# Feed-forward with a hidden width of 682: two 42-column remainders in one column block

## What is computed

```python
HID = int(DIM * 4 * 2 / 3)               # 682, DIM is 256
h = shift_token(x)
mu = h.mean(-1, keepdims=True)
var = h.var(-1, keepdims=True)
h = (h - mu) / jnp.sqrt(var + 1e-05) * lg + lb
h = h @ w1 + b1                          # w1: 256 x 1364
a, g = jnp.split(h, 2, axis=-1)          # linear half, gate
h = a * jax.nn.gelu(g, approximate=False)
x = x + h @ w2 + b2                      # w2: 682 x 256
```

## Time and profile before

| | us |
|---|---|
| median of 3 runs | 5164.81 (5160.68 to 5165.73) |
| profiled execution, span | 5174.7 |
| PE busy | 4715.5 (91%) |
| DVE busy | 3744.5 (72%) |
| ACT busy | 2880.2 (56%) |
| POOL busy | 1688.8 (33%) |
| up projection, gate blocks (L1994), 1152 matmuls | 303.2 |
| up projection, linear blocks (L1994), 1152 matmuls | 302.2 |
| down projection (L2008), 2304 matmuls | 284.9 |

### The profile page before, as it was taken

How to read it: one execution, slowest core, us unless ns; L and a number is a source line. 1 busy time by engine, 2 the same in 40 slices (tenths; PEclk the granted TensorE clock), 3 DMA queues, 4 the chain that set the end, 5 groups by cost and what they waited for, 6 DMA issues and landing times. The chain is left out here.

```text
span 5174.7 us, 97724 instructions
## 1 busy us (share of the span) xinstructions
PE 4715.5 (91%) x27802; PEld 2976.0 (58%) x27802; DVE 3744.5 (72%) x8989; ACT 2880.2 (56%) x6305; POOL 1688.8 (33%) x2440
## 2 busy tenths in 40 slices
PE   4779999999999986599999997999799999997998
PEld 2423332333323324477777775888677777776887
DVE  6978888888888849677777775554677777774554
ACT  1327666767776761366666664333566666663333
POOL 3610000000000004455555553333455555554554
PEclk8869999999999998799999998999899999998999
DMA  4753232332332317200000001111100000002221
GB/s 154 248 116 49 46 57 41 55 55 40 57 49 46 56 40 227 86 23 23 23 22 22 22 22 53 47 46 37 49 23 22 22 22 22 22 21 79 62 75 48
DMA packets 385590, 288.63 MB, mean 56 GB/s; under 512 B 64284, under 2 KB 346392, under 8 KB 385056
## 3 DMA queue, kind: packets, MB, share of 16 engines
q1 hardware_dynamic: 385056, 282.19, 22.7%
HBM read 178.74 MB, written 102.83 MB: 54 GB/s over the span
## 5 line engine op out<-in xcount | busy, mean ns | idle before, releaser
L949 DVE TENSOR_REDUCE fa_mx<-fa_pR 128x1 f32<-128x512 f32 x2048 | 1275.8, 683 | 207.1 <-PE fa_pR L826 202.1
L925 ACT ACTIVATE fa_P<-fa_pS 128x512 f32<-128x512 f32 x2048 | 1077.3, 600 | 530.1 <-PE fa_pS L849 527.0
L1558 POOL TENSOR_TENSOR wa_pn<-wa_pr,wa_ri 128x512 f32<-128x512 f32 x512 | 701.6, 1371 | 785.8 <-DVE wa_ri L1614 777.1
L826 PE MATMUL fa_pR<-fa_K,fa_Q 96*128 96x512 bf16 x2048 | 804.4, 394 | 28.9 <-DMA fa_K<-parts_d 28.4
L849 PE MATMUL fa_pS<-fa_Q,fa_K 98*128 98x512 bf16 x2048 | 784.2, 386 | 26.3 <-issue 21.8
L1179 POOL TENSOR_TENSOR ao_xn<-ao_xn,ao_mod 128x1024 f32<-128x1024 f32 x16 | 37.6, 2350 | 1739.9 <-DVE ao_xn L1144 1739.9
L1378 PE MATMUL wa_pS<-wa_kT,wa_qT 128*128 128x256 f32 x2048 | 567.3, 401 | 37.4 <-issue 34.4
L849 PEld LDWEIGHTS fa_pS<-fa_Q,fa_K 98*128 98x128 bf16 x2048 | 199.1, 98 | 637.7 <-ACT fa_P L925 439.0
L862 PE MATMUL fa_pO<-fa_P,fa_V 128*32 128x512 f32 x4096 | 551.7, 611 | 5.9 <-ACT fa_OT L914 5.2
L1495 ACT ACTIVATE wa_pr<-wa_sm,wa_mn 128x256 f32<-128x256 f32 x1024 | 512.7, 504 | 44.2 <-DVE wa_mn L1606 44.0
L1606 DVE CUSTOM_DVE_ANT_0 wa_sm<-wa_pS,wa_mask 128x256 f32<-128x256 f32 x1024 | 391.1, 419 | 143.2 <-issue 128.8
(11 more groups left out here) (191 smaller groups left out, 7547.7 us busy)
## 6 DMA issues: line engine op xcount, KB each, us to landing
parts_d<-pj_parts SPq DMA_DIRECT2D x96, 256.0 KB, 2.8
fa_Q<-parts_d SPq DMA_DIRECT2D x192, 128.0 KB, 4.5
fa_K<-parts_d SPq DMA_DIRECT2D x192, 128.0 KB, 7.2
v_d<-pj_v SPq DMA_DIRECT2D x16, 1024.0 KB, 6.0
fa_V<-v_d SPq DMA_DIRECT2D x32, 512.0 KB, 9.7
pj_x<-in_L_attn_x SPq DMA_DIRECT2D x16, 512.0 KB, 6.7
att_d<-fa_att SPq DMA_DIRECT2D x32, 256.0 KB, 3.2
ao_att<-att_d SPq DMA_DIRECT2D x16, 512.0 KB, 4.8
```

What stands on the lines that cost most here:

```text
L826: nc.tensor.matmul(row_tile(), Qs[0:SROWS, s, h, q * P:(q + 1) * P], Ks[0:SROWS, s, h, half * 512:(half + 1) * 512], start=True, stop=True ...
L925: nc.scalar.activation(Pr[:, k % 2, h, half * 512:(half + 1) * 512], pS[:, (s * exped.per + u) % T, :], ACT.Exp).then_inc(exped.sem, 1)
L949: nc.vector.tensor_reduce(mx[:, j // 2, j % 2:j % 2 + 1], row_tile(), AX.X, ALU.max).then_inc(row_free, 1)
L1558: nc.gpsimd.tensor_tensor(pn[:, hp % 2], pr[:, hp % 2], inv, ALU.mult).then_inc(s["weighted"].sem, 1)
```

## The change

The 42 last columns of the linear half and the 42 last of the gate go into one column block of `w1`: the linear ones at columns 0 to 41 of block 5, the gate ones at 64 to 105. For j = 5 PE makes this block alone, in `pG[:, 1]`, with six matmuls instead of twelve; rows 0 to 63 of it are the linear half, rows 64 to 127 the gate. ACT reads rows 64 to 127 and writes the gelu to rows 0 to 63 of `gl`; mix, `u_high` and the split of block 5 work on rows 0 to 63. Rows 64 to 127 of `u[:, :, 5]` are zeroed once for each layer. The gate half of `w1` is loaded by two transfers instead of one (640 columns and 42). `lifted` counts five for a chunk instead of six; the waits that asked for the end of the up projection by `lifted` now ask by `gated`; and PE waits for the sixth mix of the chunk before ahead of its second gate block, since that mix now reads `pG[:, 1]`.

```diff
-        gated=HB, lifted=HB, gelu=HB, mixed=HB, ...
+        gated=HB, lifted=HB - 1, gelu=HB, mixed=HB, ...
...
-        LOADS = 11
+        LOADS = 12
+        LAST = P // 2
...
+                    (w1_in[:, :, 0, 0:HID], w1_rows[:, :, 0:HID]),
+                    (w1_in[:, :, 1, 0:full], w1_rows[:, :, HID:HID + full]),
+                    (w1_in[:, :, 0, full + LAST:full + LAST + HL], w1_rows[:, :, HID + full:2 * HID]),
...
+                nc.vector.memset(u[LAST:P, :, HB - 1, :].bitcast(F32), 0.0).then_inc(zeroed, 1)
...
-                    dve.wait_ge(s["lifted"].sem, s["lifted"].upto(g(n), j + 1))
+                    if j < HB - 1:
+                        dve.wait_ge(s["lifted"].sem, s["lifted"].upto(g(n), j + 1))
...
+                    rows_, ps = (P, pA) if j < HB - 1 else (LAST, pG)
+                    nc.vector.scalar_tensor_tensor(out=uF[0:rows_, j % 2, :], in0=ps[0:rows_, j % 2, :],
+                                                   scalar=b1[0:rows_, 0, j:j + 1], in1=gl[0:rows_, j % 2, :],
...
+                            if half == 0 and j == HB - 1:
+                                continue
...
+                            if half == 1 and j == 1 and not (early(n, 1) and layer == 0):
+                                pe.wait_ge(s["mixed"].sem, s["mixed"].upto(g(n - 1)))
+                            part = half if j < HB - 1 else 0
...
+                    at, rows_ = (0, P) if j < HB - 1 else (LAST, LAST)
+                    nc.scalar.activation(gl[0:rows_, j % 2, :], pG[at:at + rows_, j % 2, :], ACT.Gelu,
+                                         bias=b1[at:at + rows_, 1, j:j + 1]).then_inc(s["gelu"].sem, 1)
```

More of the change, by code:

```diff
@@ L1727, in ffn_signals @@
         chain=LN_INCS, normed=1, biased=2, turned=1, hT_ready=2 * KT, h_split=1,
-        gated=HB, lifted=HB, gelu=HB, mixed=HB, u_high=HB, u_split=HB, y_done=1, summed=1, scaled=1, final=1,
+        gated=HB, lifted=HB - 1, gelu=HB, mixed=HB, u_high=HB, u_split=HB, y_done=1, summed=1, scaled=1, final=1,
     )
@@ L1834, in _ @@
                 ]
[L1835 to L1838, removed]
+                w1_rows = a["L0_ffn_w1"][layer].rearrange("(k p) n -> p k n", p=P)
+                loads += [
+                    (w1_in[:, :, 0, 0:HID], w1_rows[:, :, 0:HID]),
+                    (w1_in[:, :, 1, 0:full], w1_rows[:, :, HID:HID + full]),
+                    (w1_in[:, :, 0, full + LAST:full + LAST + HL], w1_rows[:, :, HID + full:2 * HID]),
+                ]
                 for d_, s_ in loads:
@@ L1846, in _ @@
                                      row[0:full].rearrange("(k p) -> p k", p=P)).then_inc(w_in, 16)
-                        sp.dma_start(b1[0:HL, half, HB - 1:HB],
+                        sp.dma_start(b1[half * LAST:half * LAST + HL, half, HB - 1:HB],
                                      row[full:HID].rearrange("(p k) -> p k", k=1)).then_inc(w_in, 16)
@@ L1888, in mix @@
                     dve.wait_ge(s["gelu"].sem, s["gelu"].upto(g(n), j + 1))
-                    dve.wait_ge(s["lifted"].sem, s["lifted"].upto(g(n), j + 1))
+                    if j < HB - 1:
+                        dve.wait_ge(s["lifted"].sem, s["lifted"].upto(g(n), j + 1))
                     if not (early(n, 1) and layer == 0 and j < 2):
                         dve.wait_ge(s["u_split"].sem, g(n) * HB + j - 1)
-                    nc.vector.scalar_tensor_tensor(out=uF[:, j % 2, :], in0=pA[:, j % 2, :], scalar=b1[:, 0, j:j + 1],
-                                                   in1=gl[:, j % 2, :], op0=ALU.add,
-                                                   op1=ALU.mult).then_inc(s["mixed"].sem, 1)
+                    rows_, ps = (P, pA) if j < HB - 1 else (LAST, pG)
+                    nc.vector.scalar_tensor_tensor(out=uF[0:rows_, j % 2, :], in0=ps[0:rows_, j % 2, :],
+                                                   scalar=b1[0:rows_, 0, j:j + 1], in1=gl[0:rows_, j % 2, :],
+                                                   op0=ALU.add, op1=ALU.mult).then_inc(s["mixed"].sem, 1)
                 def split_h(n, p):
@@ L1899, in split_h @@
                     if not early(n, 2):
-                        dve.wait_ge(s["lifted"].sem, s["lifted"].upto(g(n - 2)))
+                        dve.wait_ge(s["gated"].sem, s["gated"].upto(g(n - 2)))
                     nc.vector.tensor_tensor(hT[:, p, 1], hF[:], hT[:, p, 0].bitcast(F32),
@@ L1955, in body @@
                         pool.wait_ge(s["u_high"].sem, s["u_high"].upto(g(n), j + 1))
-                        nc.gpsimd.tensor_tensor(u[:, 1, j, :], uF[:, j % 2, :], u[:, 0, j, :].bitcast(F32),
+                        rows_ = P if j < HB - 1 else LAST
+                        nc.gpsimd.tensor_tensor(u[0:rows_, 1, j, :], uF[0:rows_, j % 2, :],
+                                                u[0:rows_, 0, j, :].bitcast(F32),
                                                 ALU.subtract).then_inc(s["u_split"].sem, 1)
@@ L1974, in _ @@
                 pe.wait_ge(w_in, 16 * LOADS)
+                pe.wait_ge(zeroed, 4)
                 def turn(n, p):
@@ L1989, in up @@
                         for half, ps, done, freed in ((1, pG, "gated", "gelu"), (0, pA, "lifted", "mixed")):
+                            if half == 0 and j == HB - 1:
+                                continue
                             if not (early(n, 1) and layer == 0 and j < 2):
                                 pe.wait_ge(s[freed].sem, g(n) * HB + j - 1)
+                            if half == 1 and j == 1 and not (early(n, 1) and layer == 0):
+                                pe.wait_ge(s["mixed"].sem, s["mixed"].upto(g(n - 1)))
+                            part = half if j < HB - 1 else 0
                             products = [(k, x, y) for k in range(KT) for x, y in SPLIT_PRODUCTS]
                             for i, (k, x, y) in enumerate(products):
-                                last = nc.tensor.matmul(ps[:, j % 2, :], w1[:, x, k, half, j * P:(j + 1) * P],
+                                last = nc.tensor.matmul(ps[:, j % 2, :], w1[:, x, k, part, j * P:(j + 1) * P],
                                                         hT[:, p, y, k, :], start=(i == 0),
@@ L2042, in h_out @@
                     if not early(n, 2):
-                        act.wait_ge(s["lifted"].sem, s["lifted"].upto(g(n - 2)))
+                        act.wait_ge(s["gated"].sem, s["gated"].upto(g(n - 2)))
                     for k in range(KT):
@@ L2052, in gelu @@
                         act.wait_ge(s["mixed"].sem, g(n) * HB + j - 1)
-                    nc.scalar.activation(gl[:, j % 2, :], pG[:, j % 2, :], ACT.Gelu,
-                                         bias=b1[:, 1, j:j + 1]).then_inc(s["gelu"].sem, 1)
+                    at, rows_ = (0, P) if j < HB - 1 else (LAST, LAST)
+                    nc.scalar.activation(gl[0:rows_, j % 2, :], pG[at:at + rows_, j % 2, :], ACT.Gelu,
+                                         bias=b1[at:at + rows_, 1, j:j + 1]).then_inc(s["gelu"].sem, 1)
                 def u_high(n, j):
@@ L2059, in u_high @@
                         act.wait_ge(s["y_done"].sem, s["y_done"].upto(g(n - 1)))
-                    nc.scalar.copy(u[:, 0, j, :], uF[:, j % 2, :]).then_inc(s["u_high"].sem, 1)
+                    rows_ = P if j < HB - 1 else LAST
+                    nc.scalar.copy(u[0:rows_, 0, j, :], uF[0:rows_, j % 2, :]).then_inc(s["u_high"].sem, 1)
                 def body(n, p, following=True):
```

## The result

The changed kernel takes 5178.0 us (18 runs, 5171.4 to 5188.1) against 5164.8 (18 runs): ratio 1.0024, 95% interval 1.0017 to 1.0030. It is slower by 13 us, with 192 matmuls fewer (27802 to 27610).

The account below looks back on a forecast made before the run. PE was taken as full in layer 0, with DVE's hn ending together with its sixth linear block, and as waiting for hn in layer 1. -2.8 + 0.9 + 5.4 = +3.5 us on 5164.8 gave 5168; range 5159 to 5176.

Parts of the forecast that it names:

- hn is what the transposes wait for: Next chunk's transposes on PE: they wait for DVE's normalized hn, so the removed 1.40 us becomes waiting; 15 chunks per layer give 0.
- The rival in which it comes off by itself: Transposes in the first layer do not wait for hn and move up, 15 x 1.40 = 21 us, some 5147; chance 0.04.
- The last chunk of each layer: No transposes there, the down projection follows directly, so the block comes off: 2 x 1.40 = 2.8 us less.
- The start of each layer: The twelfth load, issued ahead of the small vectors, delays lb by 0.47 us per layer: +0.9 us for both.
- Registers, 64 rows, the new wait: In the chunk loops: extra DVE registers, 64-row instructions and PE's wait for the previous chunk's sixth mix, all taken at 0.
- No lost clock in layer 0: PE's new waits of 1.4 us before the first layer's transposes keep the upper clock: 0.
- that rival: The first layer loses the clock too, 1.43 us in each of 15 chunks, 21.5 us: 5193; chance 0.05.
- The order of DVE and GpSimd around hn: Rival: order tips around hn; second layer 11.4 us faster (5157) or first layer 14.3 slower (5182); chance 0.03 each.
- The clock in layer 1: Second layer's waits grow to 3.2 us; 10 of 12 lose the clock instead of six, 1.43 us each: +5.4 us.

Follow-up runs that it names:

- e8: The changed kernel run once more without an edit, for a second profile: 5176.6 us, ratio 1.0019.
- e2: The changed kernel with six matmuls of unread result in place of the removed block, in both layers: 5166.5 us, ratio 0.9998.
- e6: The changed kernel with hn written one mix earlier, behind the fourth mix and before the fifth: 5133.2 us, ratio 0.9930.
- e9: The changed kernel with the whole normalization behind the first three mixes, hn before the fourth: 5100.8 us, ratio 0.9871.
- e1: The kernel before run once more without an edit, for a second profile: 5164.7 us, ratio 0.9999.
- e4: The kernel before with only the gate half of w1 loaded in two transfers instead of one: 5165.9 us, ratio 1.0003.
- e10: The kernel before with the whole normalization behind the first three mixes, hn before the fourth: 5155.6 us, ratio 0.9980.
- e3: The kernel before with six matmuls added behind the last linear block of each chunk, layer 1 alone: 5169.1 us, ratio 1.0006.
- e7: The kernel before with hn written one mix earlier, behind the fourth mix and before the fifth: 5147.4 us, ratio 0.9958.
- e5: The changed kernel with three matmuls added behind the packed block, layer 1 alone: 5169.0 us, ratio 1.0005.

## Why the prediction was wrong

The likeliest time was 5168 and the range ended at 5176; measured were 5178.0 and, in e8, 5176.6. The chance for slower by more than 0.2% was 0.09.

- **hn is what the transposes wait for: right.** In layer 0 the wait is 1.38 us (1.4 predicted), in layer 1 3.1 to 3.3 (3.2), 1.3 to 1.7 in its first three chunks (1.4 to 1.8), the offset behind hn 0.14, the chunk 26.3. e2 shows that the removed block only turned into waiting, e6 and e9 that it comes off when hn comes earlier. The rival in which it comes off by itself is out.
- **The last chunk of each layer: right.** Layer 0 takes 435.1 us in three profiles of the changed kernel or with its layer 0, and 437.0 in e1: 1.9 less, of which 1.4 is the block. The rest comes with the twelfth load: in e4, which has nothing else, the first chunk is shorter too.
- **The start of each layer: the wait right, its effect smaller.** The wait for lb is about 0.5 us longer, predicted 0.47, but the first chunk gives most of it back.
- **Registers, 64 rows, the new wait: right**, nothing that e2 can tell (up to 3 us by its interval).
- **No lost clock in layer 0: right.** The mean is 1.00, and that rival is out.
- **The order of DVE and GpSimd around hn: not tipped.** hn takes 1.38 us in layer 0 and, from the fourth chunk on, 2.3 to 2.4 in layer 1, as before. The rival mechanism is real, though: moved by one mix, in e6, hn of layer 0 takes 2.42.
- **The clock in layer 1: the step that failed.** The term was +5.4 us, put together from ten losses in place of six, at 1.43 us. Two things were wrong in it. The larger is the base: six losses came from a single execution whose span lay 9.9 us above the median of the runs. (Its time was further off: in all other profiles the time is 1.7 to 1.9 us more than the span.) The prediction said "the sum is a difference and is carried over to the median". The six losses were themselves a part of that excess: e1, e2 and e4 have one. The other is the price. Losses after waits of 1.8 us cost 1.4 to 1.7; the six of the first profile cost 1.54 in the mean, and the prediction took one pair of chunks that gives 1.43. After 3.2 us seven of seventeen cost about 2.5 (30.75 against 28.29), with the down projection at 10.61 us instead of the 9.5 that it takes after the shorter wait. The count, ten, was near: nine and eight. In sum layer 1 takes 474.8 us in the mean of the two profiles after, against 461.1 in e1: +13.7, where -1.4 + 5.4 = +4.0 was predicted.

Put together from the profiles: -1.9 in layer 0, +13.7 in layer 1, +1.0 for the waits at the starts, +12.8 us. Measured were +13.3 and +11.0 (e8).

Had the profile of before been set beside its runs at this point, the range would have shown it: a term that rests on something that changes from execution to execution needs more than one execution as a base, or the assumption that the median has none of it (one loss in place of six makes the same ten losses worth 5.7 + 5 x 1.66 = 14 us, with which the sum gives 5177). The granted clock of the runs that were not profiled fits this. Twelve of 99 runs of the kernel before took 5173 us or more; the mean clock of the whole execution is on record for eleven of them, 0.951 to 0.953, while 70 others have 0.953 to 0.956 and the first profile 0.952. The 28 runs of the changed kernel have 0.947 to 0.953. So about one execution in eight of the kernel before seems to be like the first profile. That is read from the means; at how many waits those executions lost the clock was not seen, and why one does and the next doesn't stays open.

## What to carry to other kernels

Before work is taken off a full engine, look at which instruction of another engine ends together with the piece that goes: if it ends within a tenth of a microsecond, as hn did, expect the work to turn into waiting until that one is moved too. The same packed block was worth -13 us with hn behind the fifth mix, +14 behind the fourth and +55 before it, where it also spared the kernel the new wait of e10. And where the profiled execution is longer than the median of the runs, find what it has that the others don't before counting it into the base.

## What the runs showed of the hardware

The same kernel, with the same waits of 1.8 us on PE to within 0.1 us, lost the upper clock at six of twelve of them in one execution and at one in another. How often rose with the length of the wait in these profiles, of which each run has one: none of twelve at 0.4 to 0.9 us (e3, e7, e9), one at 1.8 (e1, e2, e4; six in the first profile) and three at 1.9 (e6), seven at 2.5 (e5), eight and nine at 3.2. And a loss after the longest waits can last longer than one after the shorter: the granted clock from 4863 to 4871 in the changed kernel is 0.64 over 8 us, where in the earlier trace rows it was 0.57 over 4 and back at once.

```profile
4863.00:4871.00 8.00, 7.91 (x46) 7.92 (x47) 1.84 (x2) 3.41 (x5) 1.27 (x1) 0.64 0.00 0
```
